# A two-layer normalise-and-convolve kernel: deeper load lead for statistics units, other weights for streamed units, narrow tiles cut to their pieces

## What is computed

```python
x = x + conv(gn(x))      # gn: mean and variance over the 2 channels of a group
x = x + bias(gn(x))      # the same normalisation of the new x
# conv: causal mask (row >= column) on its input and on its output,
#       6 x 11 taps, one filter per channel
# bias: one number per channel and (row - column), from a small network of three layers
```

## Time and profile before

| | |
|---|---|
| median of 3 runs | 2638.41 us |
| the profiled execution | 2638.45 us, its span 2636.7 us |
| VectorE busy | 2304.3 us, 87% of the span |
| TensorE busy | 1979.8 us, 75% |
| ScalarE, GpSimd busy | 1660.3 and 1260.7 us, 63% and 48% |
| granted TensorE clock | 0.912 of full |
| moved by DMA | 894.88 MB, 339 GB/s over the span |

### The profile page before, as it was taken

The page is one execution under the profiler, slowest core; times in us unless marked ns, Lnnn a source line. Parts: engine busy times, 40 slices in busy tenths (PEclk is TensorE's granted clock), DMA queues, the critical chain, the costliest instruction groups (busy, mean ns, idle before and its releaser), DMA issues. The chain is left out here.

```text
span 2636.7 us, 76763 instructions
## 1 busy us (share of the span) xinstructions
PE 1979.8 (75%) x28880; PEld 1876.5 (71%) x28880; DVE 2304.3 (87%) x4175; ACT 1660.3 (63%) x3051; POOL 1260.7 (48%) x1988
## 2 busy tenths in 40 slices
PE   4289988888687876878778877888868778899800
PEld 0289887878687776877778776787768778899800
DVE  7799988899888997899888998889988899778846
ACT  2167766766576675766667666666656757687722
POOL 1123235535545454454555445554554546475543
PEclk9999998999899999999898999999889998999955
DMA  9775649999899998999989998999989997797999
GB/s 337 273 243 170 233 136 384 393 371 351 329 408 377 380 337 332 402 359 385 354 334 396 359 366 329 378 392 362 348 329 395 384 373 297 284 355 274 334 370 360
DMA packets 313546, 894.88 MB, mean 339 GB/s; under 512 B 42272, under 2 KB 42272, under 8 KB 311296
## 3 DMA queue, kind: packets, MB, share of 16 engines
q1 hardware_dynamic: 198528, 576.64, 59.3%
q10 hardware_dynamic: 114832, 316.22, 31.0%
HBM read 576.36 MB, written 316.53 MB: 339 GB/s over the span
## 5 line engine op out<-in xcount | busy, mean ns | idle before, releaser
L1184 PEld LDWEIGHTS psY<-wsplit,XT 128*128 128x128 f16 x25920 | 1607.2, 102 | 355.9 <-DVE XT L801 128.6
L1184 PE MATMUL psY<-wsplit,XT 128*128 128x168 f16 (+5 forms) x25920 | 1635.9, 223 | 290.7 <-DVE XT L801 240.2
L659 ACT CAST XT<-psT 128x512 f16<-128x512 f32 x720 | 414.8, 576 | 561.0 <-PE psT L1170 325.5
L1110 POOL COPY halo<-XT 128x16 f16<-128x16 f16 x720 | 318.9, 443 | 657.5 <-DVE XT L801 647.3
L801 DVE TENSOR_TENSOR XT<-psT,XT 128x512 f16<-128x512 f32 x720 | 493.8, 686 | 140.3 <-ACT XT L659 139.4
L1084 POOL TENSOR_TENSOR xn<-xn,mask 128x512 f32<-128x512 f32 x336 | 423.7, 1261 | 387.5 <-ACT xn L647 325.8
L829 DVE BATCH_NORM_STATS2 entries<-ring 128x6 f32<-128x512 f32 x872 | 551.4, 679 | 61.3 <-DMA ring<-in_x 61.0
L1170 PE MATMUL psT<-ident,xn 128*128 128x128 f32 x2880 | 480.3, 292 | 98.2 <-POOL xn L1084 77.6
L1119 POOL TENSOR_TENSOR ring<-ring,bias 128x1024 f32<-128x1024 f32 x181 | 408.4, 2258 | 253.7 <-ACT ring L708 253.6
L647 ACT ACTIVATE xn<-kept_c_band,normp 128x512 f32<-128x512 f32 (+2 forms) x496 | 398.4, 803 | 48.3 <-DMA kept_c_band<-in_x 26.9
L1170 PEld LDWEIGHTS psT<-ident,xn 128*128 128x128 f32 x2880 | 317.8, 146 | 107.4 <-POOL xn L1084 72.5
(11 more groups left out here) (81 smaller groups left out, 486.2 us busy)
## 6 DMA issues: line engine op xcount, KB each, us to landing
ring<-in_x SPq DMA_DIRECT2D x628, 512.0 KB, 8.6
out<-ring ACTq DMA_DIRECT2D x282, 512.0 KB, 6.1
kept_c_band<-in_x SPq DMA_DIRECT2D x224, 512.0 KB, 8.1
out<-kept_c_band ACTq DMA_DIRECT2D x224, 512.0 KB, 7.0
band<-in_x SPq DMA_DIRECT2D x48, 1024.0 KB, 11.3
out<-band ACTq DMA_DIRECT2D x45, 1024.0 KB, 8.7
ring<-out SPq DMA_DIRECT2D x90, 512.0 KB, 9.5
bias<-bias_scratch SPq DMA_DIRECT2D x16, 1793.5 KB, 8.5
```

The lines of the kernel that those rows point to most:

```text
L659: nc.scalar.copy(XT[:, n % NB3, 0, :, 2:P + 2], psT[n % NB3][:, :, :]).then_inc(hi_ready, 1)
L1110: nc.gpsimd.tensor_copy(halo[:, t, :, :, :], XT[:, n % NB3, :, :, P:P + 2]).then_inc(halo_out, 1)
L1184: last = nc.tensor.matmul(psY[m][:, 0:rows, o + lo_c:o + hi_c], XT[:, m, xp, i, 2 - sh:2 - sh + P], wsplit[:, c, wp, K * sh:K * sh + rows, ...
```

## The change

Four things. (1) `A_LEAD` is 4 in place of 2; the plan's position is still the old load position, so the load moves two positions ahead and the use stays two behind it. (2) `U_WEIGHT` is 2.2 in place of 1.8 for positions 0 to 9, 1.8 in place of 1.0 for 47 to 54, and 1.2 in place of 1.5 from 83 on. (3) Tiles narrower than 128 columns are transposed, cast, split, passed on and convolved with as many pieces as they have (2, 3 and 2). (4) The mask is applied only from where the diagonal cuts the tile. For (3) TensorE's loops take only triples whose tiles all have four pieces; the others are written straight.

```diff
+    n_pieces = [-(-min(TIN, BW * (b + 1) - STEP * t) // XC) for c, b, t in TILES]
+    left_of_diag = [max(0, BW * b - STEP * t) for c, b, t in TILES]
...
-    U_WEIGHT = lambda n: 1.8 if n < 10 else 1.5 if n > 82 else 1.0
+    U_WEIGHT = lambda n: 2.2 if n < 10 else 1.8 if 46 < n < 55 else 1.2 if n > 82 else 1.0
...
-    A_LEAD, U_LEAD, LAST_LEAD = 2, 3, 14
+    A_LEAD, U_LEAD, LAST_LEAD = 4, 3, 14
...
-    wanted = [(max(NT * g + at, NT - 1), "a", g, a) for g in range(1, G) for a, at in enumerate(STEADY.a)]
+    wanted = [(max(NT * g + at + 2 - A_LEAD, NT - 1), "a", g, a) for g in range(1, G) for a, at in enumerate(STEADY.a)]
...
-            use[kind] = max(NT * (g + 2) + planned[(g, i)], load + A_LEAD, use.get(kind, 0))
+            use[kind] = max(NT * (g + 2) + planned[(g, i)], load + 2, use.get(kind, 0))
...
-                nc.vector.tensor_tensor(XT[:, n % NB3, 1, :, 2:P + 2], psT[n % NB3][:, :, :],
-                                        XT[:, n % NB3, 0, :, 2:P + 2], ALU.subtract).then_inc(lo_ready, 1)
+                np = n_pieces[n]
+                nc.vector.tensor_tensor(XT[:, n % NB3, 1, 0:np, 2:P + 2], psT[n % NB3][:, 0:np, :],
+                                        XT[:, n % NB3, 0, 0:np, 2:P + 2], ALU.subtract).then_inc(lo_ready, 1)
...
-                    nc.vector.tensor_tensor(y, y, mask_at(b, t, c0, c1), ALU.mult).then_inc(conv_masked, 1)
+                    d0 = max(c0, left_of_diag[n])
+                    y_diag = psY[n % NB3][:, :, d0:c1]
+                    nc.vector.tensor_tensor(y_diag, y_diag, mask_at(b, t, d0, c1), ALU.mult).then_inc(conv_masked, 1)
...
-                for i in range(NPC):
+                for i in range(np):
...
-                products = [(i, sh, xp, wp) for i in range(NPC) for sh in range(3)
+                products = [(i, sh, xp, wp) for i in range(np) for sh in range(3)
...
+            def looped(j):
+
+                return all(n_pieces[(NB3 * j + i) % NT] == NPC for i in range(NB3 + 2))
...
-                with pe.Fori(1, NTC // NB3) as j:
-                    triple(first + NB3 * j, 0)
+                triples(first, 0, 1, NTC // NB3)
```

More of the change, by code:

```diff
@@ L658, in split_hi @@
                 wait(act, halo_out, N - NB3 + 1)
-                nc.scalar.copy(XT[:, n % NB3, 0, :, 2:P + 2], psT[n % NB3][:, :, :]).then_inc(hi_ready, 1)
+                np = n_pieces[n]
+                nc.scalar.copy(XT[:, n % NB3, 0, 0:np, 2:P + 2], psT[n % NB3][:, 0:np, :]).then_inc(hi_ready, 1)
             def copy_edge(g, n, w):
@@ L1080, in mask_tile @@
                 pool.wait_ge(diag_normed, ND * g + DIAG_BEFORE[n] + 1)
-                v = xn[:, n % NB3, :, :, :]
-                m = mask_at(b, t, 0, TIN)
-                m = bass.AP(m.tensor, m.offset, [m.ap[0], [-XC, NPC], [1, K], [-1, XC]])
+                i0, i1 = left_of_diag[n] // XC, n_pieces[n]
+                v = xn[:, n % NB3, i0:i1, :, :]
+                m = mask_at(b, t, XC * i0, TIN)
+                m = bass.AP(m.tensor, m.offset, [m.ap[0], [-XC, i1 - i0], [1, K], [-1, XC]])
                 nc.gpsimd.tensor_tensor(v, v, m, ALU.mult).then_inc(xn_ready, 1)
@@ L1188, in convolve, with triple, triples @@
                 last.then_inc(convolved, 1)
-            def triple(N, c, ahead=NB3, results_of=None):
+            def triple(N, c, ahead=NB3, results_of=None, first=None):
+                pieces = [NPC if first is None else n_pieces[(first + i) % NT] for i in range(NB3 + 2)]
                 for i in range(NB3):
                     if i < ahead:
-                        transpose(N + i + 2, (i + 2) % NB3)
+                        transpose(N + i + 2, (i + 2) % NB3, pieces[i + 2])
                     if i == 0 and results_of is not None:
                         sum_results(results_of)
-                    convolve(N + i, i, c)
+                    convolve(N + i, i, c, pieces[i])
+            def looped(j):
+                return all(n_pieces[(NB3 * j + i) % NT] == NPC for i in range(NB3 + 2))
+            def triples(first, c, lo, hi):
+                while lo < hi:
+                    end = lo
+                    while end < hi and looped(end):
+                        end += 1
+                    if end - lo > 1:
+                        with pe.Fori(lo, end) as j:
+                            triple(first + NB3 * j, c)
+                    else:
+                        end = lo + 1
+                        triple(first + NB3 * lo, c, first=NB3 * lo)
+                    lo = end
             def sum_means(g):
@@ L1215, in group @@
                 pe.wait_ge(w_built, chan(g, 0) + 1)
-                triple(first, 0, results_of=g - 1 if before else None)
-                with pe.Fori(1, NTC // NB3) as j:
-                    triple(first + NB3 * j, 0)
+                triple(first, 0, results_of=g - 1 if before else None, first=0)
+                triples(first, 0, 1, NTC // NB3)
                 pe.wait_ge(w_built, chan(g, 1) + 1)
-                triple(first + NTC, 1)
-                with pe.Fori(NTC // NB3 + 1, SUM1[0] if after else 2 * NTC // NB3 - 1) as j:
-                    triple(first + NB3 * j, 1)
+                triples(first, 1, NTC // NB3, SUM1[0] if after else 2 * NTC // NB3 - 1)
                 if after:
-                    triple(first + NB3 * SUM1[0], 1)
+                    triples(first, 1, SUM1[0], SUM1[0] + 1)
                     sum_means(g + 1)
-                    triple(first + NB3 * SUM1[1], 1)
+                    triples(first, 1, SUM1[1], SUM1[1] + 1)
                     sum_variances(g + 1)
-                    with pe.Fori(SUM1[1] + 1, 2 * NTC // NB3 - 1) as j:
-                        triple(first + NB3 * j, 1)
+                    triples(first, 1, SUM1[1] + 1, 2 * NTC // NB3 - 1)
             sum_means(0)
@@ L1236, in _ @@
             for g in range(1, G - 1):
-                triple(NT * g - NB3, 1)
+                triple(NT * g - NB3, 1, first=NT - NB3)
                 group(g, True, True)
-            triple(NT * (G - 1) - NB3, 1)
+            triple(NT * (G - 1) - NB3, 1, first=NT - NB3)
             group(G - 1, True, False)
-            triple(NT * G - NB3, 1, 1)
+            triple(NT * G - NB3, 1, 1, first=NT - NB3)
             sum_results(G - 1)
```

7 lines of the change are left out of this document (4 added, 3 removed).

## The result

| | before | after |
|---|---|---|
| median | 2638.33 us (2633.2 to 2640.93, 4 runs) | 2660.76 us (2654.05 to 2666.09, 4 runs) |
| profiled execution, its span | 2638.45, 2636.7 us | 2654.05, 2652.2 us |

The ratio is 1.0086, 95% interval 1.0059 to 1.0114: slower by 0.86%, where 2596 us was forecast and 2562 to 2634 given as the range. The profiled execution is the lowest of the four, 15.6 us above that of before.

The account below looks back on a forecast made before the run. It took DMA to bound the first half of a pass and VectorE most of the second. From 2638 us, -21 - 13 - 9 + 6 - 5 = -42 gave 2596 us, range 2562 to 2634.

Parts of the forecast that it names:

- Term 1: Load lead and streamed units, first half of a pass: 6.1 us wait goes, 3.5 us per pass kept, -21 us.
- rival A: Positions 5 to 39: the wait only moves, since full DMA takes back the lead's gain; 2626 us, chance 0.22.
- rival B: Ring buffers held longer stall streamed units, two stalls around positions 34 and 35 per pass; slower, 2668 us, chance 0.07.
- Term 2: Less VectorE work in split_lo and masks: 3.2 us per pass, two thirds counted, -13 us.
- Term 3: Statistics units leave positions 45 to 59 for 75 to 89, into VectorE's idle time: 1.5 us per pass, -9 us.
- Term 4: More GpSimd units beside VectorE at positions 0 to 9 and 45 to 54 slow L991: +6 us.
- Term 5: Fewer TensorE matmuls for narrow tiles, counted by half in passes 1 and 8 only: -5 us.
- Term 6: Costed at nothing: smaller ScalarE and GpSimd operations, and TensorE's straight triples, 16 per pass in place of 8.

Follow-up runs that it names:

- e17: The kernel before with only the statistics unit of position 13 issued ahead of the three kept reloads of position 10: 2631.34 us, -2.7 us (ratio 0.9989).

## Why the prediction was wrong

*Term 1 (-21) is the step that failed, and with it that its two edits stood in the sum at no cost.* It took the 6.1 us wait for time that could be kept. The wait did go: VectorE's idle time at 10 to 14 fell from 6.0 to 2.1 us per pass. But e17 removes that wait and nothing else and wins 0.5 us per pass where 3.5 were booked (2.7 us in all, with an interval of 0.5 to 5.3): the DMA engines ran at 397 GB/s behind it before and at 395 with the swap, so a consumer that comes sooner waits sooner. That is rival A, which had been given 0.22. The two other supports failed too. The 1.0 to 2.1 MB did not leave the full stretch (44.1 MB before, 44.6 after). The early weight was to empty it, and with the weights alone it moves 45.1 MB; with the lead alone it moves 42.8. And the wider distances of streamed units show no gain. A gain in the stretch itself did come with the lead alone: 5 to 39 took 108.2 us at a lead of 3 and 109.6 at 4, where it took 111.1. It was lost again right behind, at 40 to 44, which took 22.5 and 22.8 in place of 17.9.

*Neither the lead nor the early weight had a price in the sum.* That a statistics unit holds a buffer longer and pushes streamed units back stood only in rival B, as one further stall. The mechanism was right, the place was not: in the changed kernel nothing more was lost at 34 and 35 (ScalarE's waits for ring units fell from 48.0 to 10.2 us), the stall came at 40, with others at 60 and 67, and hit VectorE itself. With the lead alone both of rival B's stalls are there, ScalarE's waits of 3.6 to 4.3 us at 34 and of 4.5 to 6.0 at 40, for +29.6 us where 42 were reckoned. Rival B's time, 2668 us, is the nearest of the four, in part by luck: it still counts term 2's 13 us, and leaves the stores at 0 to 9 out. The price is measured: 29.6 us for two positions, 39.8 when both kinds have them, 84.7 for one buffer of eight, and 34.1 for the early weight, to which term 1 gave a gain.

*Term 2 (-13).* The work of the two operations fell as counted (24.4 us, 26 forecast), and with the pieces alone the time fell by 0.7 us, which is not clear of noise: most of it came back as 21.6 us more of waiting for statistics units. Two thirds were booked because they were taken to lie where VectorE is the bound. But the wait came there too: at 45 to 59, where VectorE had 0.9 us of idle time per pass, it has 2.6 with the pieces alone, and at 15 to 39 12.6 where it had 10.9.

*Term 3 (-9).* The statistics left 45 to 59 as counted (VectorE 4.4 us less there), and the stretch grew from 52.4 to 54.2, 60 to 74 from 51.4 to 53.6. Alone these two weights left the full passes as they were (312.6 us) and cost 8.3 us, most of it in pass 1. In 40 to 64 their kernel has VectorE work 3.8 us less and stand idle 4.0 more per pass. That the streamed units that took the place want buffers and stores where kept parts are stored and loaded anew is a reading, not tested.

*Term 4 (+6).* L999 takes 1467 ns on average where L991 took 1478: nothing, and the streamed units that VectorE finishes became faster. *Term 5 (-5):* pass 1 longer by 1.8 us, pass 8 shorter by 2.1: nothing in sum. With the pieces alone they are shorter by 1.2 and 1.9, no more than kernels with the old tiles differ (256.8 to 259.0 in pass 1); in the changed kernel the weights lengthen pass 1. *Term 6 (0)* fits the time of the pieces alone, but it counted wrong: the trace of a full pass has 25 of 30 triples of TensorE looped before and 16 now, so 14 are straight in place of 5, not 16 in place of 8. And TensorE's own waits did not shrink. With the pieces alone they are, for weight loads,

```profile
PEld psY L1194 <- issue: 68.3, 65, 2.3
PEld psT L1180 <- issue: 28.0, 34, 2.4
```

96.3 us together, where the kernel before has 60.0: the 54.0 of the earlier trace rows and

```profile
PEld psT L1170 <- issue: 6.0, 5, 2.0
```

Over all runs the sum is 43.9 to 78.8 us in the kernels with the old loops and 96.3 to 135.5 in the six with the new code. The new code fetches 2.02 MB of instructions on one queue in place of 0.98. The Trainium skill (Runtime: NRT & Kernel Launch, Instruction fetch mechanics) prefers straight code, since a taken branch out of the fetched window forces a fetch. These traces do not bear the preference out: the looped triples fell from 25 to 16 per pass, and the waits grew.

Of the signs named ahead, the wait at 10 to 14, the 720 fewer matmuls, VectorE's smaller work and the rate at 0 to 4 came true. The pass of 305 to 307 us did not, nor the idle time of 14 us at 5 to 39 (19.5), nor L991's longer mean. The reading that VectorE works about 283 us of each full pass fits the mean of the six, 282.3, but not the last of the two shown, 273.5.

## What to carry over

A wait for data inside a stretch where DMA runs at its ceiling is not worth its length: first ask whether bytes leave the stretch, and count them in the changed order. In a ring of few buffers a deeper lead is a price that every other user of the ring pays, in the order of the queue; try it with one buffer less, which shows at once how dear a buffer is. Weights of a planner that sit at a balance cost on either side, so each is to be moved alone. And an engine that issues stores between its own instructions pays for them with the next one: count the stores ahead of whatever the others wait for.

## What was not expected of the hardware

Positions 10 to 14 moved 403 to 413 GB/s, as a mean over the full passes, in every kernel with whole loads, whatever the order. With half the bytes of the statistics loads it was still 397 GB/s there in the kernel before (383 in the changed one), and the median time from issue to landing fell only from 8.6 us for all ring loads to 7.0 for the halved ones and 6.5 for the whole ones. Issuing one of the ring's stores held ScalarE for 0.33 to 1.81 us in the kernel before, and for up to 1.90 in that of the early weight. More straight code on TensorE, 14 triples a pass in place of 5, raised its weight loads' waits for the sequencer from 60.0 to 96.3 us; with the smaller tiles together it changed the time by less than can be told.
